# A three-layer kernel on one Trainium2 core: the spectral stage's direct taps in split parts, eight reversing products, and an earlier first image pair

## What is computed

```
x   = deformable_conv3x3(x) + residual, on 8 images of 64 channels
x   = x + attention(layernorm(x)),     16 heads, rotary positions, causal
u   = layernorm(x) as tokens
out = x + sum_k (phi_k * u) @ Mix_k    (16 causal filters over time, odd and even lags apart)
        + sum_i shift(u, i) @ Mu_i     (3 direct taps, i = 0, 1, 2)
```

## Time and profile before

| | before |
|---|---|
| median of 3 runs | 2921.23 us |
| the profiled execution | 2919.81 us |
| its span | 2917.9 us |
| PE busy | 2744.6 us (94%) |
| DVE busy | 2184.7 us (75%) |
| POOL busy | 1734.4 us (59%) |
| mean granted TensorE clock | 0.969 |

### The profile page before, as it was taken

The page is one execution under the profiler, slowest core; times in us unless marked ns, Lnnn a source line. Parts: engine busy times, 40 slices in busy tenths (PEclk is TensorE's granted clock), DMA queues, the critical chain, the costliest instruction groups (busy, mean ns, idle before and its releaser), DMA issues. The chain is left out here.

```text
span 2917.9 us, 60678 instructions
## 1 busy us (share of the span) xinstructions
PE 2744.6 (94%) x18761; PEld 1791.2 (61%) x18761; DVE 2184.7 (75%) x3909; ACT 1329.2 (46%) x1788; POOL 1734.4 (59%) x1827
## 2 busy tenths in 40 slices
PE   3639999999999999999999999999999899999998
PEld 1334655655655655655565565565565788888887
DVE  3457888888788788878878887887888675767676
ACT  1103444444444444444444444444444465656565
POOL 3746777777777777777777777777776860000000
PEclk8658999999999999999999999999999999999999
DMA  5543222222222222222222222235354643434343
GB/s 148 142 120 77 65 63 54 73 60 62 68 60 62 66 61 63 62 65 63 59 67 63 59 64 67 56 63 70 55 65 62 171 145 120 153 123 145 117 157 103
DMA packets 160412, 249.21 MB, mean 85 GB/s; under 512 B 71662, under 2 KB 94526, under 8 KB 160350
## 3 DMA queue, kind: packets, MB, share of 16 engines
q1 hardware_dynamic: 126990, 156.66, 19.3%
q0 software_dynamic: 33360, 91.66, 13.5%
HBM read 230.65 MB, written 17.04 MB: 85 GB/s over the span
## 5 line engine op out<-in xcount | busy, mean ns | idle before, releaser
L1146 ACT ACTIVATE attention_probs<-attention_pss 128x1024 f32<-128x1024 f32 x576 | 589.6, 1024 | 311.6 <-PE attention_pss L983 299.1
L1352 POOL DMA_INDIRECT attention_gat<-table,attention_idx x585 | 556.9, 952 | 200.2 <-issue 126.6
L983 PE MATMUL attention_pss<-attention_kq 64*128 64x512 f32 (+3 forms) x3072 | 651.9, 483 | 0.0
L1213 DVE TENSOR_REDUCE attention_mx_half<-attention_pss 128x2 f32<-128x1024 f32 (+3 forms) x520 | 513.0, 1019 | 98.7 <-PE attention_pss L983 98.7
L1085 PE MATMUL attention_psY<-attention_probs,attention_xt 128*64 128x512 f32 (+3 forms) x3120 | 574.1, 496 | 0.2 <-issue 0.2
L1645 DVE SCALAR_TENSOR_TENSOR spectral_eo<-spectral_psE,kept_sig,spectral_eo 64x512 fp32r<-64x512 f32 x512 | 383.9, 750 | 169.6 <-ACT spectral_eo L1616 163.4
L1309 POOL TENSOR_TENSOR attention_kq<-attention_tA,attention_tB 128x512 f32<-128x512 f32 x260 | 416.2, 1611 | 114.6 <-DVE attention_tB L1223 105.6
L1534 PE MATMUL spectral_psE<-spectral_tz,spectral_up 128*128 128x512 f32 (+1 forms) x2304 | 460.4, 357 | 0.0
L983 PE MATMUL attention_pss<-attention_rows_m,attention_ones 64*128 64x512 f32 (+2 forms) x1536 | 458.8, 530 | 0.0
L1616 ACT ACTIVATE spectral_eo<-spectral_psE,kept_sig 64x512 fp32r<-64x512 f32 x512 | 349.8, 683 | 237.5 <-PE spectral_psE L1534 232.5
L1534 PEld LDWEIGHTS spectral_psE<-spectral_tz,spectral_up 128*128 128x128 f32 x2304 | 385.1, 189 | 72.0
(11 more groups left out here) (195 smaller groups left out, 3198.7 us busy)
## 6 DMA issues: line engine op xcount, KB each, us to landing
spectral_tz<-phis SPq DMA_DIRECT2D x128, 320.5 KB, 4.6
spectral_tz<-phis SPq DMA_DIRECT2D x128, 320.0 KB, 4.3
attention_xb<-xn SPq DMA_DIRECT2D x132, 256.0 KB, 3.8
attention_gat<-table,attention_idx POOLq DMA_INDIRECT x585
table<-front_pixT SPq DMA_DIRECT2D x32, 288.0 KB
attention_wt<-in_w SPq DMA_DIRECT2D x66, 128.0 KB, 3.6
attention_xt<-xt SPq DMA_DIRECT2D x18, 128.0 KB, 2.2
attention_xs<-in_x SPq DMA_DIRECT2D x65, 32.0 KB
```

The source lines that it names most:

```text
L983: ins = pe.matmul(out(n), left(rows), right(rows), **flags)
L1146: act.activation(probs[:, u[1], :, :].rearrange("p n q -> p (n q)"), pss[:, slot, :], ACT.Exp, scale=float(E) ** -0.5).then_inc(s_act, 1)
L1213: ins = dve.tensor_reduce(mx[:, :, i] if i < 4 else mx_half[:, :, i - 4, k0 // 4], scores, AX.X, ALU.max)
L1352: pool.indirect_dma_start(gat[:, n, :, :].rearrange("p q c -> p (q c)"), None, d.table.rearrange("r q c -> r (q c)"), bass.IndirectOffsetO ...
```

## The change

In the front stage `mixs` is no longer cleared. The first image pair, `pair_avg`, `ident`, `offw` and `offb` are loaded first, the other pairs next, and the scales' inputs behind them. The moments are made twice, for pair 0 alone and then for pairs 1 to 3; between them lie `pad(0)` and the scales. PE's `pixels(0)` goes between the taps of `conv(0)`, as do the two averages of the other pairs. POOL splits `mixu` into a high and a low part, straight into `mixs`; the trip through memory is gone. ACT copies `perm` to float32r at the end of attention.

In the spectral stage `uT` has two images apart, each as high part in its own 64 rows and low part (by DVE) in the other 64; the direct taps are 15 float32r products, 128 by 128. The reversing products are 8 in float32r, of tokens that POOL (before pair 0: ACT and DVE) splits into `split`. What opens a pair (`begin`) stands before `mix_in(15)` of the pair before; the taps stand behind `conv(0)`. ACT copies the lower sums by segment into `fin`, and DVE adds into it there. The last pair is a copy of the body outside the loop, without normalization and `begin`. SP loads the next pair's first two filters before it stores the result.

```diff
-                pool.memset(m.mixs[:, :, :, :, :], 0.0).then_inc(s_zero, 1)
...
-                sp.dma_start(lw[:, :], d.logw.partition_broadcast(P)).then_inc(s_small, 16)
...
-                sp.dma_start(pair_avg[:, :], d.pair_avg).then_inc(s_const, 16)
+                sp.dma_start(m.X[:, 0, :], d.x[0:2].rearrange("b c h w -> (b c) (h w)")).then_inc(s_x0, 16)
+                sp.dma_start(pair_avg[:, :], d.pair_avg).then_inc(s_avgw, 16)
+                sp.dma_start(m.ident[:, :], d.ident).then_inc(s_ident, 16)
                 for h in range(2):
                     sp.dma_start(offw[64 * h:64 * h + 64, :, 18 * h:18 * h + 18], d.offw).then_inc(s_offw, 16)
...
+                for g in range(1, G):
+                    sp.dma_start(m.X[:, g, :], d.x[2 * g:2 * g + 2].rearrange("b c h w -> (b c) (h w)")).then_inc(s_x, 16)
+                sp.dma_start(lw[:, :], d.logw.partition_broadcast(P)).then_inc(s_small, 16)
...
-                sp.dma_start(d.mixu, m.mixu[:, :, :, :]).then_inc(s_mst, 16)
...
+                do(pool.tensor_copy(m.mixs[:, :, :, 0, :], m.mixu[:, :, :, :]))
+                do(pool.tensor_tensor(m.mixs[:, :, :, 1, :], m.mixu[:, :, :, :], m.mixs[:, :, :, 0, :].bitcast(F32), ALU.subtract))
...
+                def moments(first, last, count):
+                    for g in range(first, last):
+                        for h in range(2):
+                            ins = dve.bn_stats(gn_stats[:, g, h, :], m.X[:, g, h * HB:(h + 1) * HB])
...
+                dve.wait_ge(s_x0, 16)
+                moments(0, 1, 0)
                 pad(0)
+                each = Chain(dve, s_weights)
+                dve.wait_ge(s_small, 32)
...
+                dve.wait_ge(s_x, 16 * (G - 1))
+                moments(1, G, 1)
                 pad(1)
+                dve.wait_ge(s_const, 32)
                 draw(0)
                 draw(1)
...
+                        if g == 0 and tap in (0, 2, 4):
+                            pixels(0, range(4 * (tap // 2), min(4 * (tap // 2) + 4, NCH)))
+                        if g == 0 and tap == 5:
+                            averages(1, 1, G)
+                        if g == 0 and tap == 8:
+                            squares(1, 1, G)
...
-                pe.wait_ge(s_const, 64)
+                pe.wait_ge(s_avgw, 16)
+                averages(0, 0, 1)
+                squares(0, 0, 1)
+                pe.wait_ge(s_ident, 16)
                 pe.wait_ge(s_offw, 96)
...
                 for g in range(2):
                     conv(g)
-                    pixels(g)
+                    if g:
+                        pixels(g)
                     offsets(g)
...
+                act.wait_ge(s_sq, 2)
+                act.activation(dev[:, 0:1], gn_var[:, 0:1], ACT.Sqrt).then_inc(s_std, 1)
                 act.wait_ge(s_ex, 1)
                 act.activation(soft[:, :], lw[:, :], ACT.Exp).then_inc(s_soft, 1)
+                pixels(0)
+                act.wait_ge(s_sq, 4)
+                act.activation(dev[:, 1:G], gn_var[:, 1:G], ACT.Sqrt).then_inc(s_std, 1)
+                act.wait_ge(s_offw, 96)
+                offsets(0)
+                offsets(1)
+                pixels(1)
...
+                act.wait_ge(s_ahead, 16 * 5)
+                act.activation(m.perm[:, :, :, :], perm_f[:, :, :, :], ACT.Copy)
...
-        low = sb("low", [C, 4 * HB])
+        split = sb("split", [P, 2, NT, 2, C], F32R)
...
+                for k in range(2):
+                    lags(0, k)
+                with sp.Fori(0, G - 1) as g:
+                    for k in range(2, KF):
+                        lags(g, k)
+                    for k in range(2):
+                        lags(g + 1, k)
+                    result(g)
+                for k in range(2, KF):
+                    lags(G - 1, k)
+                result(G - 1)
                 sp.wait_ge(s_out, 16 * G + 16)
 
...
-                    pool.wait_ge(s_mix, KF * g + (KF + 2))
+                    pool.wait_ge(s_mix, KF * g + 3)
                     raw(2 * g + 3)
+                    pool.wait_ge(s_un, 2 * g + 2)
+                    wait_apart(pool, s_upps, g + 1, s_apart)
+                    pool.tensor_copy(split[:, 0, :, :, :], un[:, :, :, :]).then_inc(s_split, 1)
+                    wait_apart(pool, s_split, 2 * g + 3, s_apart)
+                    pool.tensor_tensor(split[:, 1, :, :, :], un[:, :, :, :], split[:, 0, :, :, :].bitcast(F32),
+                                       ALU.subtract).then_inc(s_split, 1)
 
...
+                def begin(n, more=True):
+                    if more:
+                        pe.wait_ge(s_un, 2 * n)
+                    for t in range(NT):
+                        if t % 4 == 0:
+                            pe.wait_ge(s_lo, 64 * n + (t // 4 + 1))
+                        ins = pe.transpose(psE[:, t // 4, (t % 4) * P:(t % 4) * P + P],
+                                           un[:, t].rearrange("p b c -> p (b c)"), m.ident[:, :])
+                    ins.then_inc(s_uTps, 1)
+                    pe.wait_ge(s_split, 2 * n + 2)
+                    for p in range(2):
+                        pe.wait_ge(s_lo, 64 * n + (p + 3))
+                        for x in range(2):
+                            for h in range(2):
+                                ins = pe.matmul(psE[:, 2 + p, :], perm[:, p, x, :],
+                                                split[:, h, x:NT:2, :, :].rearrange("p a b c -> p a (b c)"),
+                                                start=(x == 0 and h == 0), stop=(x == 1 and h == 1))
+                    ins.then_inc(s_upps, 1)
+                def pair(g, more):
...
-                    pe.wait_ge(s_un, 2 * g + 2)
-                    pe.wait_ge(s_lo, 64 * g + 4)
...
-                    for p in range(2):
-                        for a in range(4):
-                            for x in range(2):
-                                ins = pe.matmul(psE[:, 2 + p, a * P:(a + 1) * P], perm[:, p, x, :],
-                                                un[:, 2 * a + x].rearrange("p b c -> p (b c)"), start=(x == 0), stop=(x == 1))
-                    ins.then_inc(s_upps, 1)
+                    pe.wait_ge(s_uTl, g + 1)
+                    pe.wait_ge(s_pad, 1)
+                    pe.wait_ge(s_up, g + 1)
+                    pe.wait_ge(s_upl, g + 1)
+                    conv(0)
 
                     pe.wait_ge(s_fin, g + 1)
-                    pe.wait_ge(s_uT, g + 1)
-                    pe.wait_ge(s_pad, 1)
-                    for c, (lo, hi, scales) in enumerate(SEGMENTS):
...
-                                    pe.matmul(segment(c, slice(C * p, C * p + C))[:, 2 * p + b, :], mixu[:, b, scales, i, 0:C],
-                                              uT[:, f:f + 2 * (hi - lo) - 1:2],
...
+                    for i in range(3):
+                        for c, (lo, hi, scales) in enumerate(SEGMENTS):
+                            f = 2 - i + 2 * lo
+                            taps = uT[:, :, f:f + 2 * (hi - lo)].rearrange("q b (n p) -> q p b n", p=2)
+                            for p in ((slice(0, 2),) if hi - lo <= P else (slice(0, 1), slice(1, 2))):
+                                pe.matmul(segment(c)[:, 2 * p.start:2 * p.stop, :].rearrange("q (p b) n -> q p b n", b=2),
+                                          mixu[:, scales, i, :, :].rearrange("q h c -> q (h c)"), taps[:, p],
+                                          start=(i == 0 and c != 1), stop=False, skip_group_check=True)
                     pe.wait_ge(s_traw, g + 1)
...
-                    pe.wait_ge(s_up, g + 1)
-                    pe.wait_ge(s_upl, g + 1)
-                    for k in range(KF):
+                    for k in range(1, KF):
                         conv(k)
-                        if k:
-                            mix_in(k - 1)
+                        mix_in(k - 1)
+                    if more:
+                        begin(g + 1)
                     mix_in(KF - 1)
+                begin(0, more=False)
+                with pe.Fori(0, G - 1) as g:
+                    pair(g, True)
+                pair(G - 1, False)
...
+                def begin(n):
+                    act.wait_ge(s_uTps, n + 1)
+                    for b in range(2):
+                        rows = slice(C * b, C * b + C)
+                        ins = act.activation(uT[rows, b, 2:2 + S], psE[rows, 0:2, :].rearrange("p a n -> p (a n)"), ACT.Copy)
+                    ins.then_inc(s_uT, 1)
...
-                    act.wait_ge(s_mix, KF * g + KF + 2)
-                    act.activation(low[:, :], acc[C:P, :], ACT.Copy).then_inc(s_low, 1)
+                    if more:
+                        begin(g + 1)
+                    act.wait_ge(s_mix, KF * g + (KF + 2))
+                    act.wait_ge(s_out, 16 * g + 16)
+                    for c, (lo, hi, _) in enumerate(SEGMENTS):
+                        act.activation(fin[:, :, lo:hi, :].rearrange("c b n a -> c a b n"),
```

(25 more changed lines are left out.)

200 lines of the change are left out of this document (87 added, 113 removed).

## The result

| | before | after |
|---|---|---|
| median | 2919.98 us (5 runs) | 2904.86 us (5 runs, 2903.16 to 2907.78) |
| span of the profiled execution | 2917.9 us | 2901.4 us |
| mean granted clock | 0.969 | 0.968 |

The ratio is 0.9946, with an interval from 0.9931 to 0.996. The kernel is 15.1 us faster, by more than the 0.2% that can be told. The forecast was 31.9 us and 2889.3, with a range to 2903: the sign holds, half of the gain doesn't, and the median lies 1.9 us above the range. Two more executions of the kernel before moved its median from 2921.23 to 2919.98 us.

A forecast was written before the change was run, and what follows sets the result against it. PE was taken to bound the kernel, busy 94% of the span, with the front stage and spectral joints open. 16.4 + 18.0 - 3.3 + 0.8 = 31.9 us off 2919.8, plus 1.4 for the median, gave 2889.3 us, range 2878 to 2903.

The forecast's parts named there:

- What bounds it, and where: Whole kernel: PE bounds it, busy 94% of the span; what is open lies in front stage and spectral joints.
- Term 1: Front stage: POOL starts at 35.5 us instead of 51.88, a gain of 16.4 us, bounds 13 and 19.
- Rival (a): Front stage: indices or offw transfers come last, not the table; gain 11 us, 2895 us; chance 0.10.
- Term 2: Three joints between pairs in the spectral stage: 12.1 us each in place of 18.1, a gain of 18.0 us.
- M: In a joint of the spectral stage, the end of mix_in(14); conv(0) was forecast to start at M + 7.1.
- the choice of 2.9 us for fifteen taps: Direct taps behind conv(0): float32r reads a step of two as fast as a unit step, 2.9 us instead of 5.63.
- rival (b): Direct taps: the stepped reading halves float32r, 2.7 us for each of four pairs, 2900 us; chance 0.09.
- rival (d): Each pair's conv(0), taps and raw tokens: clock stays slow after idling, 48 us lost, 2937 us; chance 0.04.
- the row of 0.62: Profile row at 2432 us, granted clock 0.62 after 1.92 us idle, cited for a slow clock after idle stretches.
- Term 3: Pair 0 of the spectral stage: conv(0) 3.6 us earlier, but taps and slow clock follow; net loss 3.3 us.
- Term 4: The kernel's end: DVE's last add starts when ACT's four copies by segments are done, a gain of 0.8 us.
- Rivals (c) and (e): (c) front stage's gain half lost behind POOL, 2897 us, chance 0.07; (e) joints shorten less, 2898 us, chance 0.08.

The follow-up runs named there:

- experiment 9: The kernel before with the changed front stage alone, save for the clearing of mixs and the trip of mixu: 2908.61 us, ratio 0.9965.
- experiments 1 and 4: Changed kernel with direct taps reading at unit step (other tokens' values): 2893.9 us; changed kernel, whole, with even and odd tokens of uT apart: 2895.98 us.
- experiment 3: The kernel before with its float32 direct taps reading tokens at a step of one instead of two (other tokens' values): 2918.4 us against 2919.5.
- experiment 5: The changed kernel with ten more products by a zero matrix filling PE's idle stretch in the three joints: 2901.05 us, ratio 0.9936.

## Why the prediction was half right

- **What bounds it, and where**: right. From the first product of the attention stage to the start of the spectral stage it is 2060.1 us in both profiles (210.58 to 2270.66, 194.16 to 2254.27), and all that moved lies in the places named.
- **Term 1, the front stage, 16.4 us**: right in the profiled execution (the index copy at 35.21, forecast 35.5), but partly by luck, for errors of its steps cancel: SP's table writes began at 21.61 and not 22.7, and from there to the copy it took 13.6 us and not 12.84, because the indices, given 0.9 us of slack, had none; where the table came last it took 13.5 to 14.1. In other profiles the gain is up to 2.7 us smaller (experiment 9). Rival (a) was true in its mechanism and small in its size: up to 1.4 us, and not 5.
- **Term 2, the joints, 18.0 us**: here it failed; 6.7 came (conv(1) to conv(1) 157.2 us three times, before 160.1, 159.1 and 159.2). The way to conv(0) was right to 0.1 us (M + 7.04). The step that failed is the choice of 2.9 us for fifteen taps between the ends 2.9 and 5.63. The far end, that of rival (b), is the measured one, 5.55. It costs 2.65 us in each of four pairs, 8.0 in the joints and 10.6 in all, and experiments 1 and 4 gained 11.0 and 8.9 by taking it away. I chose by float32 rows; those were read rightly (experiment 3) and say nothing of float32r. This was the rival that was given 0.09. The Trainium skill (SBUF — State Buffer, the note on cachelines) has a step of up to four float32 elements at full rate. The measurement of this reader, float32r at a step of two, is 632 ns against 399; it differs, and it decides. The other part is rival (d), held at 0.04 and only in its extreme form: 1.5 us a joint, 4.6 in all, of which experiment 5 gave 3.8 back by doing more work. Its mechanism was right where its price was not: the clock doesn't stay low through the raw tokens, but it is low for some 3 us of conv(0), and 6 in pair 0. The forecast had priced this in pair 0 and at nothing in the joints, although 2.4 us of idle time stood in its own sum and the row of 0.62 followed 1.92 us. Taps and clock leave 5.4 of the 18.0; most of what is missing up to 6.7 is the first joint of the kernel before, 0.9 us longer than the 159.2 reckoned with.
- **Term 3, pair 0, a loss of 3.3 us**: the loss was 7.8 (conv(1) 29.9 us after the start instead of 22.1). By its steps: nine matrices took 6.3 us instead of 5.2, so conv(0) came after 12.5 us and not 11.4; the slow clock cost 2.8 and not 2; the taps 2.65. Unseen was the transfer of the first filter, 10 to 11 us behind the start, which would have stood next.
- **Term 4, the end, 0.8 us**: 1.2.
- **Sum**: 16.4 + 6.7 - 7.8 + 1.2 = 16.5, which is the difference of the two profiled spans. Rivals (c) and (e) did not happen.

What stays open: why a float32r product runs at half rate with a step (only steps of two and four were tried, in one kernel), and why the clock fell in 11 joints and not in 4 with the same idle time. Open too is why the same front stage gives between 13.7 and 16.4 us from profile to profile.

## What to carry to other kernels

When a product changes its type, none of its old prices comes along, and least of all that an access pattern was free. It may be that the slower product hides what the fast one shows, but no run here tests that. Lay data out so that float32r reads its moving operand with a unit step, and let the copy out of the PSUM do the reordering, which cost nothing here. And cost each new wait on PE twice, for its length and for the slow clock behind it; it is worth reordering so that what the next product needs first is made first, but look what becomes late next: here it was a transfer, then DVE's queue.
